# Step orders of five engines rewritten in a float32 attention kernel, on one core

## The chip, the cores and the metric

The kernel runs on one core of a Trainium2 chip. The metric is the device time of one execution in microseconds (us), as the median of several runs; lower is better. The engines of the core are named as in the profile: PE is TensorE (PEld its weight loads), DVE is VectorE, ACT is ScalarE, POOL is GpSimd, SP is SyncE, which here only issues DMAs.

## The reference

For each of 8 batches of 512 rows and 1024 columns, in float32 (the constants `EPS = 1e-6`, 16 heads of 64):

```python
scale_shift = emb @ W_emb + b_emb
scale, shift = jnp.split(scale_shift, 2, axis=-1)
xn = _rms_norm(x, g_norm) * (1.0 + scale) + shift
qkv = xn @ W_qkv
q = _rms_norm(q, g_q)
k = _rms_norm(k, g_k)
logits = jnp.einsum('bhqd,bhkd->bhqk', q, k) * d ** (-0.5)
attn = jax.nn.softmax(logits, axis=-1)
o = jnp.einsum('bhqk,bhkd->bhqd', attn, v)
return o + o @ W_out        # and x is added to it
```

## The kernel before

The work is a stream of small steps, 8 batches one behind the other, each batch with 8 pairs of heads. Precision is kept by splitting numbers in a high and a low part: a projection is three matmuls (high by high, high by low, low by high), a score or a value product is two.

What each engine does, and in which order, is written out by hand as text: three tables `HEAD` (batch 0, lines 34 to 94), `BODY` (batches 1 to 6, lines 96 to 141, run six times) and `TAIL` (batch 7, lines 143 to 180), each with one list of steps for each of the five engines. A step is named pair, letter, number: `3F2` is step F number 2 of pair 3. Pairs 8 and 9 in a table are pairs 0 and 1 of the batch that follows, so the batches overlap. A list is followed strictly; semaphores hold an engine where its next step needs another engine. The letters:

- **C** and **P** (PE, lines 500 to 502 and 525 to 527): six matmuls of a projection, 128x384 (for P 32 to 47 128x256). C is the q, k, v projection of a pair, P the output projection, which has 48 steps a batch and few companions on the other engines.
- **D** on ACT copies v and squares q and k (lines 741, 742), on DVE sums the squares (L880), on POOL adds an epsilon and takes the power -0.5 (L970, L973, 128x4 each); **M** on DVE scales q and k out of the projection bank (L886).
- **T** (PE, L553) turns q (T0) and k (T1); ACT rounds them (L696, L700), DVE makes the rest (L830, L834).
- **S** (PE, lines 590, 591): two 128x512 matmuls of scores. DVE takes the row maximum (L859), ACT the exponential with its sum (L718, two instructions). **N** on DVE: reciprocal of the sum (L863), and the scaling of the row block of `probs` in place, from SBUF to SBUF, 128x512 (L865).
- **F** (PE, L598): four 128x128 transposes of the scaled probabilities into one of two flip banks. ACT rounds them to `pt_hi` (L724), DVE subtracts to `pt_lo` (L869) and by that frees the bank. A flip (F, T or X) waits until the flip two before it has been freed (`releases`, line 238).
- **W** (PE, lines 609, 610): the two value products of an F; it waits until that F has been freed. **V** splits v for it (ACT L688, POOL L951, 128x256).
- **O** adds the two halves of a head's result (ACT L729, DVE L876). **Q** splits the pair's result: ACT rounds it (`o_hi`, L734), POOL subtracts (`o_lo`, L966, 128x512).
- **X** and **A** make the next batch's normalised input (ACT L648, L660, L666; DVE L784, L796; POOL L960, 128x512). **L** splits the weights, in batch 0 alone: ACT L643, and the remainder half on DVE (L767) and half on POOL (L933), 128x384, both with two operands in SBUF. **Y** is a step like L in batch 0 (L854). **K** and **R** add the residual (L907).

The two instructions of a W step:

```python
                        pe.wait_ge(flip_free, flip_at(order, b, "F", n, p)[0] + 1)
                        v_t = v_split[h][:, i, :]
                        nc.tensor.matmul(pv_bank[h][:, :], v_t, pt_hi[n % 2][:, :], start=(i == 0), stop=False)
                        nc.tensor.matmul(pv_bank[h][:, :], v_t, pt_lo[n % 2][:, :], start=False,
                                         stop=(i == TT - 1)).then_inc(pv_used, 1)
```

Of the kernel before, what the change touches and what calls it, by code (L numbers as in the profile page):

```python
# [50 lines left out]
        8W4 8W5 P5 P6 8F6 P7 P8 P9 8F7 8W6 9S0 9S1 P10 8W7 P11 9S2 9S3 P12 P13 P14 9S4 9S5 P15 9F0 9F1 9S6 9S7 P16 9F2
        9W0 9F3 9W1 P17 P18 9W2 9W3 P19 P20 P21 9F4 9F5 P22 P23 9F6 9F7 9W4 9W5 P24 P25 9W6 9W7 P26 P27 P28 P29 P30 P31
# [1098 lines left out]
```

## Time and profile before

| what | value |
|---|---|
| median of 3 runs | 2278.25 us (2277.76 to 2278.84) |
| the profiled execution's own time | 2278.89 us |
| its span, first to last instruction | 2276.0 us |
| PE busy | 2256.2 us (99%), 13392 matmuls |
| DVE busy | 1597.9 us (70%) |
| ACT busy | 1345.7 us (59%) |
| POOL busy | 651.7 us (29%) |
| granted TensorE clock, mean | 0.999 |

The span is what the timeline shows; the execution's own time is 2.9 us more, which lies around it. Busy time of PE is a union of matmuls whose ends are modelled, so 99% does not say that PE never waits; the starts of its instructions do.

### The profile page before, as it was taken

To read this page: it belongs to the slowest core of one execution; us is meant where nothing else is said; L and a number is where in the kernel's file an instruction comes from. 1 tells how busy PE (TensorE), PEld (TensorE's weight loads), DVE (VectorE), ACT (ScalarE), POOL (GpSimd) and SP (SyncE) were. 2 spreads that over 40 slices of the span, in tenths; PEclk is the share of its full clock that TensorE was granted. 3 is DMA by queue.
4 is the path that set the end of the run, shared out by engine and by line. 5 is a ranking of instruction groups with operands and counts; after the bars stand their busy time and mean duration, and the time that the engine had idled before them with its cause. 6 is when DMAs were issued, how large, how long until landed. Compare 5 with 4: busy or idle time off the path is not lost.

```text
span 2276.0 us, 36733 instructions
## 1 busy us (share of the span) xinstructions
PE 2256.2 (99%) x13392; PEld 2110.3 (93%) x13392; DVE 1597.9 (70%) x3284; ACT 1345.7 (59%) x3101; POOL 651.7 (29%) x880
## 2 busy tenths in 40 slices
...
GB/s 359 224 167 177 112 154 228 178 99 110 118 220 184 107 115 88 256 148 112 111 114 256 112 112 112 122 253 107 112 112 130 291 92 118 82 151 246 111 121 65
DMA packets 71269, 346.35 MB, mean 152 GB/s; under 512 B 7601, under 2 KB 43441, under 8 KB 47537
## 3 DMA queue, kind: packets, MB, share of 16 engines
...
## 4 chain that ended last, share of the span: by engine, by line
PE 86%; DVE 8%; ACT 2%; issue 1%; POOL 0%; DMA 0%; ACTq 0%; DVEq 0%
PE proj_bank L502 18%; PE proj_bank L500 18%; PE proj_bank L501 18%; PE flip_bank L598 9%; PE pv_bank L609 5%; PE pv_bank L610 5%; PE score_bank L590 4%; PE score_bank L591 4%; PE flip_bank L553 2%; DVE probs L865 2%; DVE neg_max L859 2%; DVE pt_lo L869 2%; PE flip_bank L563 1%; ACT k_hi L700 1%; PE proj_bank L525 1%
## 5 line engine op out<-in xcount | busy, mean ns | idle before, releaser
L500 PE MATMUL proj_bank<-w_split,xn_hi 128*128 128x384 f32 x2048 | 700.0, 342 | 1.4 <-DVE res L907 0.8
L502 PE MATMUL proj_bank<-w_split,xn_lo 128*128 128x384 f32 x2048 | 688.5, 336 | 0.0
L501 PE MATMUL proj_bank<-w_split,xn_hi 128*128 128x384 f32 x2048 | 687.4, 336 | 0.0
L718 ACT ACTIVATE probs<-score_bank,neg_max 128x512 f32<-128x512 f32 x512 | 352.6, 691 | 213.5 <-DVE neg_max L859 211.2
L500 PEld LDWEIGHTS proj_bank<-w_split,xn_hi 128*128 128x128 f32 x2048 | 385.2, 188 | 18.1 <-DVE xn_lo L854 1.0
L501 PEld LDWEIGHTS proj_bank<-w_split,xn_hi 128*128 128x128 f32 x2048 | 385.5, 188 | 15.2
L724 ACT CAST pt_hi<-flip_bank 128x512 fp32r<-128x512 f32 x512 | 288.8, 591 | 182.0 <-PE flip_bank L598 91.1
L869 DVE TENSOR_TENSOR pt_lo<-flip_bank,pt_hi 128x512 fp32r<-128x512 f32 x512 | 339.9, 685 | 78.1 <-ACT pt_hi L724 75.9
L502 PEld LDWEIGHTS proj_bank<-w_split,xn_lo 128*128 128x128 f32 x2048 | 384.8, 188 | 0.0
L859 DVE TENSOR_REDUCE neg_max<-score_bank 128x1 f32<-128x512 f32 x512 | 341.3, 684 | 17.0 <-PE score_bank L591 13.0
L865 DVE TENSOR_SCALAR probs<-probs,row_inv 128x512 f32<-128x512 f32 x512 | 275.7, 539 | 18.1
L598 PE MATMUL flip_bank<-ident,probs 128*128 128x128 f32 x2048 | 284.4, 273 | 1.1 <-DVE q_split L830 0.4
L598 PEld LDWEIGHTS flip_bank<-ident,probs 128*128 128x128 f32 x2048 | 242.5, 140 | 32.8 <-DVE pt_lo L869 7.3
L973 POOL TENSOR_TENSOR qk_rstd<-qk_ms_eps,neg_half 128x4 f32<-128x4 f32 x256 | 264.6, 1033 | 20.0
L970 POOL TENSOR_TENSOR qk_ms_eps<-qk_ms,eps_col 128x4 f32<-128x4 f32 x256 | 55.3, 216 | 719.2 <-DVE qk_ms L880 719.1
L609 PE MATMUL pv_bank<-pt_hi,v_split 128*128 128x512 f32 x512 | 224.3, 438 | 4.2 <-DVE pt_lo L869 4.2
L500 PE MATMUL proj_bank<-w_split,o_hi 128*128 128x384 f32 (+1 forms) x672 | 215.2, 320 | 0.0
L951 POOL TENSOR_TENSOR v_split<-v_stage,v_split 128x256 fp32r<-128x256 f32 x128 | 98.9, 773 | 401.3 <-ACT v_split L688 401.3
L502 PE MATMUL proj_bank<-w_split,o_lo 128*128 128x384 f32 (+1 forms) x672 | 213.6, 318 | 0.0
L501 PE MATMUL proj_bank<-w_split,o_hi 128*128 128x384 f32 (+1 forms) x672 | 213.5, 318 | 0.0
L590 PE MATMUL score_bank<-k_hi,q_split 128*128 128x512 f32 x512 | 206.0, 402 | 0.1
L591 PE MATMUL score_bank<-k_lo,q_split 128*128 128x512 f32 x512 | 201.6, 394 | 0.0
...
## 6 DMA issues: line engine op xcount, KB each, us to landing
...
```

Source lines behind the costliest of these rows:

```text
L500: nc.tensor.matmul(dst, a_hi, w_hi, start=(kt == 0), stop=False)
L501: nc.tensor.matmul(dst, a_hi, w_lo, start=False, stop=False)
L502: mm = nc.tensor.matmul(dst, a_lo, w_hi, start=False, stop=(kt == KT - 1))
L590: nc.tensor.matmul(score_bank[n % 2][:, :], q_t, k_hi[h][:, :], start=True, stop=False)
L591: nc.tensor.matmul(score_bank[n % 2][:, :], q_t, k_lo[h][:, :], start=False, stop=True).then_inc(score_full, 1)
L598: mm = nc.tensor.transpose(flip_bank[flip][:, qt * P:(qt + 1) * P], probs[h][:, qt, i * P:(i + 1) * P], ident[:, :])
L609: nc.tensor.matmul(pv_bank[h][:, :], v_t, pt_hi[n % 2][:, :], start=(i == 0), stop=False)
L718: nc.scalar.activation(probs[h][:, i, :], score_bank[n % 2][:, :], ACT.Exp, bias=neg_max[:, n:n + 1], accum_out=row_sum[:, n:n + 1]).then_ ...
L724: nc.scalar.copy(pt_hi[n % 2][:, :], flip_bank[flip][:, :]).then_inc(flip_hi, 1)
L859: nc.vector.tensor_reduce(neg_max[:, n:n + 1], score_bank[n % 2][:, :], AX.X, ALU.max, negate=True).then_inc(max_done, 1)
L865: nc.vector.tensor_scalar(probs[h][:, i, :], probs[h][:, i, :], row_inv[:, n:n + 1], None, ALU.mult).then_inc(probs_ready, 1)
L869: nc.vector.tensor_tensor(pt_lo[n % 2][:, :], flip_bank[flip][:, :], f32(pt_hi[n % 2][:, :]), ALU.subtract).then_inc(flip_free, 1)
```

## The change

The functions, the instructions, the jobs and the buffers stay. The text of the orders changes: each of the 14 lists that changed holds the same steps as before, in another order (in `TAIL`, the list of SyncE did not change). By its description the orders were planned with wide GpSimd steps and VectorE steps on two SBUF operands kept apart.

Cut to its core, the start of the lists of `BODY`, one place of `BODY` and `HEAD` that the prediction names, and the lists of POOL and SP in `BODY`:

```diff
 BODY = {
     "TensorE": """
         2C0 2C1 2C2 2C3 2C4 2C5 2C6 2C7 2C8 2C9 2C10 2C11 2C12 2C13 2C14 2C15 3C0 3C1 3C2 3C3 2T0 2T1 3C4 3C5 3C6 3C7
-        3C8 3C9 2S0 2S1 3C10 3C11 2S2 2S3 3C12 3C13 3C14 2S4 2S5 3C15 2F0 2F1 4C0 2S6 2S7 4C1 2F2 2F3 2W0 2W1 4C2 4C3
-        4C4 3T0 3T1 2W2 2W3 4C5 4C6 4C7 2F4 4C8 4C9 2F5 3S0 2F6 2W4 3S1 4C10 2F7 2W5 3S2 3S3 2W6 4C11 2W7 4C12 3S4 3S5
-        3F0 3F1 4C13 4C14 3F2 3W0 3F3 3W1 3S6 3S7 3W2 4C15 3W3 5C0 5C1 3F4 3F5 5C2 5C3 4T0 4T1 3W4 3W5 5C4 5C5 3F6 5C6
...
-        8S6 8F0 8F1 9C14 9C15 8F2 8F3 8W0 8W1 8S7 P0 8W2 8W3 9T0 9T1 P1 P2 P3 P4 8F4 P5 P6 8F5 8F6 8W4 9S0 9S1 8F7 8W5
...
+        3C8 3C9 2S0 2S1 3C10 3C11 2S2 2S3 3C12 3C13 3C14 2S4 2S5 3C15 2F0 2F1 4C0 2S6 4C1 2W0 2W1 2S7 2F2 2F3 4C2 4C3
+        3T0 3T1 2W2 2W3 4C4 4C5 2F4 4C6 4C7 4C8 2F5 2W4 2F6 3S0 3S1 2F7 2W5 2W6 4C9 4C10 2W7 3S2 3S3 4C11 4C12 3S4 3S5
+        4C13 3F0 3F1 4C14 3S6 3W0 3S7 3W1 3F2 3F3 4C15 5C0 3W2 3W3 5C1 3F4 3F5 5C2 5C3 4T0 4T1 3W4 3W5 5C4 5C5 3F6 5C6
...
+        9C12 8S6 8W0 8S7 8W1 8F2 8F3 9C13 9C14 8W2 8W3 9C15 8F4 8F5 P0 P1 8W4 9T0 9T1 8W5 P2 P3 P4 8F6 P5 P6 8F7 8W6 9S0
...
     "ScalarE": """
...
-        2F2 2F3 4D0 3T0 3V0 3T1 4D1 2F4 2O0 2F5 3S0 2F6 3S1 2F7 3S2 3S3 4D2 3V1 2O1 3F0 3S4 3F1 3S5 2Q0 3F2 3F3 3S6 4D3
...
+        2F3 2S7 4D0 3T0 3V0 3T1 2F4 2O0 4D1 2F5 2F6 2F7 3S0 3S1 2O1 3V1 3S2 3S3 4D2 2Q0 3S4 3F0 3F1 3S5 3F2 3F3 3S6 3S7
...
     "VectorE": """
...
-        2F6 3N1 2F7 3S2 3S3 3N2 3N3 4D2 3S4 2O1 3S5 3F0 4M2 3F1 3N4 3N5 3F2 3S6 3F3 3S7 3N6 4D3 3N7 3O0 4M3 3F4 3F5 5D0
...
+        2F7 3N0 3N1 3S2 3S3 2O1 3N2 3N3 4D2 3S4 3S5 3N4 3F0 3F1 4M2 3N5 3S6 3S7 3F2 3F3 3N6 3N7 4D3 3O0 4M3 3F4 3F5 5D0
...
     "GpSimd": """
-        0Q0 1Q0 2D0 2D1 2D2 2V0 2D3 2V1 3D0 3D1 +A0 +A1 3D2 +A2 +A3 3D3 4D0 3V0 4D1 3V1 4D2 2Q0 4D3 4V0 5D0 5D1 4V1 3Q0
-        5D2 5D3 5V0 6D0 6D1 5V1 4Q0 6D2 6D3 6V0 7D0 +X0 +X1 7D1 7D2 +X2 +X3 6V1 7D3 +X4 +X5 5Q0 8D0 +X6 +X7 8D1 8D2 7V0
-        7V1 8D3 6Q0 9D0 9D1 8V0 8V1 9D2 7Q0 9D3 9V0 9V1""".split(),
+        0Q0 1Q0 2D0 2D1 2D2 2V0 2D3 2V1 3D0 3D1 +A0 +A1 3D2 +A2 +A3 3D3 4D0 3V0 4D1 3V1 2Q0 4D2 4D3 4V0 5D0 5D1 4V1 3Q0
+        5D2 5D3 5V0 6D0 6D1 5V1 4Q0 6D2 6D3 6V0 7D0 6V1 +X0 +X1 7D1 5Q0 7D2 +X2 +X3 7D3 +X4 +X5 8D0 8D1 +X6 +X7 7V0 8D2
+        7V1 8D3 6Q0 8V0 9D0 9D1 8V1 7Q0 9D2 9D3 9V0 9V1""".split(),
     "SyncE": """
-        E2 E3 E4 3W1 E5 4W0 4W1 +X0 +X1 +X2 +X3 5W0 5W1 6W0 6W1 7W0 7W1 8W0 8W1 9W0 9W1 W0 W1 W2 W3 O0 E6 O1 E7 O2 E8 W4
+        E2 E3 E4 3W1 E5 4W0 4W1 +X0 +X1 +X2 +X3 5W0 5W1 6W0 6W1 7W0 7W1 8W0 8W1 9W0 9W1 W0 W1 W2 W3 O0 E6 O1 E7 O2 W4 E8
```

And of `HEAD`, TensorE:

```diff
-        2C12 1S4 1S5 1F0 1F1 2C13 2C14 1F2 1W0 1F3 1W1 1S6 1S7 1W2 2C15 1W3 3C0 3C1 1F4 1F5 3C2 3C3 2T0 2T1 1W4 1W5 3C4
...
+        7C12 7C13 6S6 7C14 6S7 6F0 7C15 6F1 8C0 8C1 6W0 +X2 6W1 8C2 8C3 7T0 8C4 7T1 8C5 8C6 8C7 6F2 8C8 8C9 8C10 +X3 6W2
+        7S0 7S1 6F3 8C11 6F4 6W3 6F5 6W4 6F6 7S2 7S3 8C12 6F7 6W5 6W6 8C13 8C14 6W7 7S4 7S5 8C15 7F0 7F1 7S6 9C0 7S7 9C1
```

## Rows read from the trace of the kernel before

**Rows 1.** The page: span, busy time by engine, and two groups of instructions.
```profile
span 2276.0 us, 36733 instructions
...
PE 2256.2 (99%) x13392; PEld 2110.3 (93%) x13392; DVE 1597.9 (70%) x3284; ACT 1345.7 (59%) x3101; POOL 651.7 (29%) x880
...
L724 ACT CAST pt_hi<-flip_bank 128x512 fp32r<-128x512 f32 x512 | 288.8, 591 | 182.0 <-PE flip_bank L598 91.1
...
L865 DVE TENSOR_SCALAR probs<-probs,row_inv 128x512 f32<-128x512 f32 x512 | 275.7, 539 | 18.1
```

**Rows 2.** Timeline of PE, batch 3: start us, us, engine, line, tiles, count.
```profile
1005.74 1.04 PE L598 MATMUL flip_bank<-ident,probs 128*128 128x128 f32 x8
...
1006.78 0.34 PE L501 MATMUL proj_bank<-w_split,xn_hi 128*128 128x384 f32 x1
1006.96 0.34 PE L502 MATMUL proj_bank<-w_split,xn_lo 128*128 128x384 f32 x1
...
1008.53 0.34 PE L502 MATMUL proj_bank<-w_split,xn_lo 128*128 128x384 f32 x1
```

**Rows 3.** The same timeline, around the wait of 3W2.
```profile
1010.97 0.40 PE L590 MATMUL score_bank<-k_hi,q_split 128*128 128x512 f32 x1
1011.20 0.40 PE L591 MATMUL score_bank<-k_lo,q_split 128*128 128x512 f32 x1
1012.20 0.50 PE L609 MATMUL pv_bank<-pt_hi,v_split 128*128 128x512 f32 x1 [0.60 <-DVE pt_lo L869]
```

**Rows 4.** Timelines of ACT, POOL and DVE ahead of the wait of rows 3.
```profile
1008.67 0.64 ACT L734 CAST o_hi<-o_pair 128x512 fp32r<-128x512 f32 x1
...
1009.38 1.29 POOL L966 TENSOR_TENSOR o_lo<-o_pair,o_hi 128x512 fp32r<-128x512 f32 x1 [2.10 <-ACT o_hi L734]
...
1009.38 1.58 DVE L865 TENSOR_SCALAR probs<-probs,row_inv 128x512 f32<-128x512 f32 x1
...
1011.46 0.68 DVE L869 TENSOR_TENSOR pt_lo<-flip_bank,pt_hi 128x512 fp32r<-128x512 f32 x1
```

**Rows 5.** Timelines of POOL, DVE and PE, around the wait of 8F2 in batch 3.
```profile
1154.57 1.28 POOL L966 TENSOR_TENSOR o_lo<-o_pair,o_hi 128x512 fp32r<-128x512 f32 x1 [0.69 <-ACT o_hi L734]
...
1155.12 1.02 DVE L865 TENSOR_SCALAR probs<-probs,row_inv 128x512 f32<-128x512 f32 x1
...
1157.56 0.34 PE L502 MATMUL proj_bank<-w_split,xn_lo 128*128 128x384 f32 x1
1157.98 1.25 PE L598 MATMUL flip_bank<-ident,probs 128*128 128x128 f32 x8
1158.99 0.47 PE L609 MATMUL pv_bank<-pt_hi,v_split 128*128 128x512 f32 x1
```

**Rows 6.** Waits of PEld in batch 3 (943.1 to 1221.5): total us, times, longest.
```profile
PEld flip_bank L598 <- DVE pt_lo L869: 1.1, 4, 0.4
```

**Rows 7.** The same view for batch 0 (41 to 387).
```profile
PEld flip_bank L553 <- DVE pt_lo L869: 2.3, 4, 1.8
PEld pv_bank L609 <- DVE pt_lo L869: 1.6, 3, 1.0
```

**Rows 8.** Timelines of POOL, DVE and PE in batch 0, around the wait of 8T1.
```profile
292.68 4.90 POOL L933 TENSOR_TENSOR w_split<-w_raw,w_split 128x384 fp32r<-128x384 f32 x4 [1.22 <-ACT w_split L643]
...
294.06 3.94 DVE L767 TENSOR_TENSOR w_split<-w_raw,w_split 128x384 fp32r<-128x384 f32 x3
...
296.83 0.34 PE L502 MATMUL proj_bank<-w_split,xn_lo 128*128 128x384 f32 x1
298.65 0.66 PE L553 MATMUL flip_bank<-ident,qk_stage 128*128 128x128 f32 x4 [1.48 <-DVE pt_lo L869]
```

**Rows 9.** Line L865 by itself: ns min/median/max, first and last start.
```profile
L865 DVE TENSOR_SCALAR probs<-probs,row_inv x512: 485/487/1585, 76.1 to 2240.8; 128x512 f32<-128x512 f32 x171
```

**Rows 10.** Timelines of POOL and DVE in batch 0: a power beside L865.
```profile
226.31 1.01 POOL L973 TENSOR_TENSOR qk_rstd<-qk_ms_eps,neg_half 128x4 f32<-128x4 f32 x1
...
227.13 0.49 DVE L865 TENSOR_SCALAR probs<-probs,row_inv 128x512 f32<-128x512 f32 x1
```

More of the change, by code:

```diff
@@ L51 @@
[L51 to L52 removed]
+        1C5 1C6 1C7 1C8 1C9 0S0 0S1 1C10 1C11 0S2 0S3 1C12 1C13 0S4 0S5 1C14 0F0 0F1 1C15 0S6 2C0 0W0 0W1 0S7 0F2 0F3
+        2C1 2C2 2C3 1T0 1T1 0W2 0W3 2C4 2C5 2C6 0F4 2C7 2C8 2C9 0W4 0F5 0F6 1S0 1S1 2C10 0F7 0W5 0W6 2C11 1S2 1S3 0W7
+        2C12 2C13 1S4 2C14 1S5 1F0 1F1 2C15 1S6 3C0 1W0 1W1 1S7 1F2 1F3 3C1 3C2 3C3 1W2 2T0 2T1 1W3 3C4 3C5 3C6 1F4 3C7
@@ new lines @@
+        3C8 3C9 1W4 1F5 1F6 2S0 2S1 3C10 3C11 1F7 1W5 1W6 2S2 2S3 3C12 1W7 3C13 3C14 3C15 4C0 2S4 2S5 4C1 2F0 2F1 4C2
+        2S6 4C3 2W0 2W1 3T0 3T1 2S7 4C4 4C5 4C6 4C7 2F2 4C8 4C9 2F3 2W2 3S0 2F4 3S1 2W3 2F5 4C10 2W4 2F6 3S2 4C11 3S3
+        2F7 2W5 2W6 4C12 3S4 4C13 2W7 3S5 3F0 3F1 4C14 3S6 4C15 3W0 3W1 3S7 3F2 3F3 5C0 5C1 3W2 4T0 4T1 3W3 5C2 5C3 5C4
+        5C5 5C6 3F4 3F5 4S0 4S1 5C7 3W4 3F6 3F7 3W5 5C8 4S2 3W6 4S3 5C9 3W7 5C10 4S4 5C11 4S5 5C12 4F0 4F1 4S6 4S7 5C13
+        5C14 4W0 4W1 4F2 4F3 5C15 6C0 4F4 4W2 4W3 4F5 6C1 6C2 5T0 5T1 4W4 4W5 6C3 6C4 6C5 4F6 6C6 6C7 4F7 4W6 5S0 5S1
@@ L53 @@
+        9C11 7W6 7W7 9C12 9C13 8S4 8S5 9C14 8F0 8F1 9C15 8S6 P0 8W0 8W1 8S7 8F2 8F3 P1 P2 P3 9T0 9T1 8W2 8W3 P4 P5 P6
+        8F4 P7 P8 8F5 9S0 9S1 8W4 8F6 P9 8F7 8W5 8W6 9S2 9S3 P10 8W7 P11 9S4 P12 9S5 P13 9S6 9F0 9F1 P14 P15 9W0 9W1 9S7
+        9F2 9F3 P16 P17 9W2 9W3 P18 9F4 9F5 P19 P20 9W4 9W5 9F6 9F7 P21 P22 9W6 9W7 P23 P24 P25 P26 P27 P28 P29 P30 P31
         P32 P33 P34 P35 P36 P37 P38 P39 P40 P41 P42 P43 P44 P45 P46 P47""".split(),
@@ new lines @@
+        0S1 1D2 0S2 0S3 0S4 0F0 0F1 0S5 1D3 3L0 3L1 3L2 0S6 0F2 0F3 3L3 2D0 0S7 1T0 1V0 1T1 0F4 0O0 2D1 0F5 0F6 1S0 0F7
+        1S1 2D2 0O1 1V1 1S2 1S3 0Q0 1S4 1F0 1F1 1S5 2D3 4L0 4L1 4L2 1F2 1F3 1S6 1S7 4L3 +A0 3D0 2T0 2V0 2T1 1F4 1O0 3D1
+        +A1 +A2 1F5 1F6 +A3 2S0 3D2 2S1 1F7 1O1 2V1 1Q0 2S2 2S3 3D3 5L0 5L1 5L2 2S4 2F0 2F1 2S5 5L3 4D0 2S6 3T0 3T1 2S7
+        2F2 4D1 2F3 2F4 3S0 2F5 3V0 2O0 3S1 2F6 4D2 3S2 2F7 3S3 2O1 3S4 3F0 3F1 3S5 3V1 2Q0 4D3 6L0 3S6 3F2 3S7 3F3 6L1
+        6L2 4T0 4V0 4T1 5D0 6L3 3O0 3F4 3F5 5D1 3F6 4S0 3F7 4S1 4S2 3O1 4S3 4V1 3Q0 5D2 4S4 4S5 4F0 4F1 4S6 4S7 4F2 4F3
@@ new lines @@
+        5D3 7L0 7L1 4F4 5V0 4F5 7L2 7L3 4O0 5T0 5T1 6D0 4F6 6D1 4F7 4O1 5S0 5S1 5V1 4Q0 5S2 5S3 6D2 5S4 5F0 5F1 5S5 5S6
+        5F2 5S7 5F3 6D3 5F4 6V0 5O0 5F5 6T0 6T1 7D0 5F6 5F7 6S0 7D1 6S1 5O1 +X0 6V1 5Q0 6S2 6S3 7D2 6S4 6S5 +X1 6F0 7D3
+        6F1 6S6 6S7 +X2 8D0 7T0 7T1 6F2 8D1 +X3 6F3 6F4 7S0 7S1 7V0 8D2 6F5 6O0 6F6 6F7 7S2 7S3 6O1 7V1 7S4 7S5 7F0 7F1
+        8D3 L0 L1 L2 7S6 7F2 7S7 7F3 L3 9D0 6Q0 8T0 8V0 8T1 7O0 9D1 7F4 7F5 8S0 8S1 7F6 7F7 9D2 8S2 7O1 8S3 8V1 7Q0 8S4
+        8F0 8F1 8S5 9D3 L4 L5 L6 8S6 8F2 8F3 L7 8S7 9T0 9V0 9T1 8F4 8O0 8F5 8F6 9S0 9S1 8F7 9S2 8O1 9S3 9V1 9S4 9F0 9F1
@@ new lines @@
+        9S5 9S6 L8 L9 L10 L11 9F2 9F3 9S7 9O0 9F4 9F5 9F6 9F7 9O1""".split(),
+    "VectorE": """
+        X0 Y0 X1 1L0 1L1 1L2 Y1 X2 0D0 1L3 0M0 Y2 X3 0D1 0M1 Y3 0D2 0M2 0D3 2L0 0M3 2L1 2L2 1D0 2L3 0T0 1M0 0T1 1D1 0S0
+        0S1 1M1 0N0 0N1 0S2 1D2 0S3 0N2 1M2 0N3 0S4 0S5 0N4 0F0 0F1 0N5 1D3 0S6 3L0 3L1 3L2 1M3 0F2 0F3 0S7 2D0 3L3 0N6
+        0N7 1T0 2M0 1T1 0F4 2D1 0O0 2M1 0F5 0F6 1S0 1S1 1N0 0F7 1N1 2D2 1S2 1S3 0O1 2M2 1N2 1N3 1S4 1S5 1N4 1F0 1F1 1N5
+        2D3 1S6 1S7 4L0 4L1 4L2 1F2 1F3 2M3 4L3 1N6 1N7 3D0 2T0 +A0 3M0 2T1 1F4 3D1 1O0 3M1 2S0 1F5 1F6 2S1 2N0 +A1 3D2
+        2N1 1F7 +A2 3M2 +A3 1O1 2S2 2S3 2N2 2N3 3D3 2S4 2S5 5L0 5L1 5L2 2F0 2F1 3M3 2S6 4D0 5L3 2N4 2N5 4M0 3T0 2S7 2N6
+        3T1 2F2 4D1 2N7 2F3 3S0 4M1 2F4 3S1 3N0 2F5 2O0 3N1 2F6 3S2 4D2 3S3 3N2 2F7 4M2 3N3 3S4 3S5 2O1 3N4 3F0 3F1 3S6
+        4D3 3S7 6L0 3N5 3F2 4M3 3F3 6L1 6L2 4T0 3N6 3N7 4T1 5D0 3O0 6L3 3F4 3F5 5M0 4S0 5D1 4S1 3F6 4N0 3F7 5M1 4N1 4S2
+        4S3 4N2 3O1 4N3 4S4 4S5 5D2 4N4 4N5 4F0 4F1 5M2 4S6 4S7 4N6 4N7 4F2 4F3 5D3 +B0 7L0 7L1 5M3 4F4 4F5 7L2 4O0 5T0
+        7L3 5T1 4F6 6D0 6D1 4F7 6M0 5S0 5S1 6M1 4O1 5N0 5N1 5S2 5S3 I0 5N2 5N3 6D2 5S4 5S5 6M2 5N4 5F0 5F1 5N5 5S6 5S7
+        5N6 5F2 5N7 5F3 6D3 5F4 6M3 5O0 5F5 6T0 6T1 5F6 7D0 5F7 6S0 7M0 6S1 +X0 7D1 6N0 6N1 5O1 7M1 6S2 6S3 6N2 6N3 7D2
+        6S4 6S5 +X1 7M2 6S6 6N4 6N5 6S7 6F0 7D3 6F1 6N6 6N7 +X2 7M3 8D0 7T0 8M0 7T1 6F2 8D1 +X3 8M1 7S0 7S1 6F3 6F4 7N0
+        8D2 6F5 6O0 6F6 8M2 7N1 7S2 6F7 7S3 7N2 7N3 7S4 7S5 6O1 7N4 7N5 7F0 7F1 8D3 7S6 7S7 L0 L1 L2 7F2 8M3 7F3 L3 9D0
+        7N6 8T0 9M0 7N7 8T1 9D1 7O0 7F4 8S0 7F5 9M1 8S1 8N0 I1 8N1 7F6 7F7 8S2 8S3 9D2 8N2 7O1 8N3 9M2 8S4 8S5 8N4 8F0
+        8F1 8N5 9D3 8S6 L4 L5 L6 9M3 8F2 8F3 8S7 R0 L7 8N6 8N7 9T0 9T1 R1 8F4 8O0 8F5 9S0 9S1 8F6 I2 9N0 8F7 9N1 9S2 9S3
+        9N2 R2 9S4 8O1 9N3 9N4 9S5 9S6 9F0 9F1 9N5 R3 9N6 L8 L9 L10 9S7 9F2 9F3 L11 9N7 9F4 9F5 R4 9F6 9F7 R5 R6 R7 R8
@@ L89 @@
-        L4 L5 L6 L7 9V0 9V1 L8 L9 L10 L11""".split(),
+        X1 1L0 1L1 X3 1L2 0D0 1L3 X5 0D1 X7 0D2 0D3 0V0 2L0 1D0 2L1 2L2 2L3 0V1 1D1 1D2 3L0 1D3 3L1 3L2 3L3 2D0 1V0 2D1
+        2D2 1V1 0Q0 4L0 2D3 4L1 4L2 +A0 4L3 2V0 3D0 3D1 +A1 +A2 +A3 3D2 2V1 1Q0 5L0 3D3 5L1 5L2 5L3 4D0 4D1 3V0 4D2 3V1
+        2Q0 4D3 6L0 6L1 6L2 4V0 6L3 5D0 5D1 4V1 3Q0 5D2 5D3 7L0 5V0 7L1 7L2 7L3 6D0 6D1 5V1 4Q0 6D2 6D3 6V0 7D0 7D1 +X0
+        6V1 +X1 7D2 5Q0 +X2 +X3 7D3 +X4 8D0 +X5 8D1 +X6 +X7 7V0 8D2 7V1 L0 8D3 L1 L2 L3 9D0 8V0 6Q0 9D1 9D2 8V1 7Q0 L4
@@ new lines @@
+        7C3 5F7 7C4 7C5 7C6 +X0 5W7 6S0 6S1 7C7 7C8 +X1 7C9 6S2 6S3 7C10 7C11 6S4 6S5 7C12 7C13 +X2 7C14 6S6 6S7 7C15
+        8C0 8C1 6F0 8C2 8C3 6F1 8C4 7T0 6W0 6W1 7T1 8C5 8C6 6F2 8C7 8C8 8C9 +X3 6W2 7S0 7S1 6F3 8C10 8C11 6F4 7S2 6W3
+        6F5 7S3 6W4 6F6 8C12 6F7 6W5 7S4 7S5 6W6 8C13 6W7 7F0 7F1 8C14 7S6 8C15 7W0 7W1 7S7 7F2 7F3 9C0 9C1 8T0 7W2 8T1
+        7W3 9C2 9C3 7F4 9C4 9C5 9C6 7F5 7W4 7F6 8S0 8S1 7F7 7W5 7W6 9C7 9C8 7W7 8S2 8S3 9C9 9C10 8S4 8S5 9C11 8F0 8F1
+        9C12 8S6 8W0 8S7 8W1 8F2 8F3 9C13 9C14 8W2 8W3 9C15 8F4 8F5 P0 P1 8W4 9T0 9T1 8W5 P2 P3 P4 8F6 P5 P6 8F7 8W6 9S0
@@ L122 @@
+        6V0 5O0 5F5 5F6 6T0 6T1 5F7 7D0 5O1 6V1 +X0 6S0 6S1 7D1 5Q0 6S2 6S3 7D2 +X1 6S4 6S5 6S6 6S7 7D3 +X2 6F0 8D0 6F1
+        7T0 7T1 6F2 8D1 +X3 6F3 7S0 6F4 7S1 8D2 7V0 6F5 7S2 6O0 6F6 7S3 6F7 7S4 7F0 7F1 7S5 6O1 7V1 8D3 7S6 6Q0 7F2 7S7
+        7F3 8T0 8V0 8T1 7F4 9D0 7O0 7F5 7F6 7F7 8S0 8S1 9D1 7O1 8V1 8S2 8S3 7Q0 8S4 8F0 8F1 8S5 9D2 8F2 8F3 8S6 8S7 8O0
+        9D3 8F4 8F5 9V0 9T0 9T1 8F6 8F7 9S0 9S1 8O1 9V1 9S2 9S3 9F0 9S4 9F1 9S5 9S6 9F2 9S7 9F3 9F4 9O0 9F5 9F6 9F7 9O1""".split(),
     "VectorE": """
@@ new lines @@
+        5F0 5F1 5N5 6D2 5S6 5S7 6M2 5N6 5F2 5N7 5F3 6D3 5F4 5O0 5F5 6M3 5F6 6T0 6T1 5F7 7D0 +X0 7M0 6S0 6S1 5O1 6N0 6N1
+        7D1 6S2 6S3 +X1 7M1 7D2 6S4 6N2 6N3 7M2 6S5 6N4 6N5 6S6 6S7 +X2 6N6 7D3 6N7 7M3 6F0 8D0 6F1 7T0 8M0 7T1 6F2 8D1
+        +X3 8M1 7S0 7S1 6F3 7N0 6F4 7S2 8D2 7S3 6F5 7N1 7N2 6F6 8M2 7N3 6F7 7S4 6O0 7S5 7N4 7F0 7F1 7N5 7S6 6O1 8D3 7S7
+        7N6 7F2 8M3 7F3 7N7 8T0 8T1 7F4 9D0 7O0 7F5 9M0 7F6 8S0 8S1 7F7 8N0 8N1 9D1 8S2 8S3 9M1 7O1 8N2 8N3 8S4 8S5 8N4
+        8F0 8F1 8N5 9D2 8S6 8S7 8F2 8F3 9M2 8N6 8N7 8O0 9D3 8F4 8F5 9M3 9T0 R0 9T1 8F6 8F7 9S0 9S1 R1 9N0 9N1 8O1 9S2
@@ new lines @@
+        2W2 3T1 2W3 4C3 4C4 2F4 4C5 4C6 4C7 2F5 2W4 2F6 3S0 3S1 2F7 2W5 2W6 4C8 4C9 2W7 3S2 3S3 4C10 4C11 3S4 3S5 4C12
+        3F0 3F1 3S6 4C13 3S7 4C14 3W0 3W1 3F2 3F3 4C15 5C0 3F4 3W2 3W3 3F5 5C1 3W4 4T0 5C2 4T1 3W5 5C3 5C4 3F6 5C5 5C6
+        3F7 3W6 4S0 4S1 5C7 3W7 5C8 4S2 5C9 4S3 5C10 4S4 5C11 4S5 5C12 4S6 4F0 4F1 5C13 5C14 4W0 4W1 4S7 4F2 4F3 5C15
+        6C0 4F4 4W2 4W3 4F5 6C1 4W4 5T0 6C2 5T1 4W5 6C3 6C4 4F6 6C5 6C6 4F7 4W6 5S0 5S1 6C7 4W7 6C8 5S2 6C9 5S3 6C10 5S4
+        6C11 5S5 6C12 5S6 5F0 5F1 6C13 6C14 5W0 5W1 5S7 5F2 5F3 6C15 7C0 5F4 5W2 5W3 5F5 7C1 5W4 6T0 7C2 6T1 5W5 7C3 7C4
```

133 lines of the change are left out of this document (38 added, 95 removed).

## Prediction

> **What bounds the kernel now.** I read the page first. PE is busy for 2256.2 of 2276.0 us, DVE, the next, for 1597.9 [rows 1]. So the span is PE's stream of 13392 matmuls, and only two things can change it: the pace of the stream, and the places where PE stands still. Neither is seen in PE's busy share, because a matmul's end is modelled. Both are seen in the starts, so I read PE's timeline.
>
> The pace: nine projection matmuls of 384 columns start from 1006.96 to 1008.53 [rows 2], 0.174 us each, and a C or P step of six takes 1.05 us. A matmul of 512 columns takes 0.23 (1010.97 to 1011.20) [rows 3], an S or W step 0.46. Eight transposes and one projection matmul fill 1005.74 to 1006.78 [rows 2]; less 0.17 that is 0.87, so an F step of four costs 0.44. Wherever PE's starts stand further apart than this, it waited.
>
> The waits: in batch 3 there are two places of weight. **3W2**: the last score matmul starts at 1011.20, the value product should start at 1011.43 and starts at 1012.20 [rows 3]: 0.77 us. **8F2**: after the projection matmul of 1157.56 the flips should start at 1157.74 and start at 1157.98, and these eight take 1.01 us up to the next start where 0.87 is their price [rows 5]: 0.24 + 0.14, some 0.4. All waits of PEld for `pt_lo` at flips in this batch come to 1.1 us in four [rows 6], which holds 8F2; weight loads run up to a quarter of a microsecond ahead of their matmuls, so PE itself loses less. I put the batch at 0.77 + 0.4 + 0.4 for the small ones, 1.6 us. The same two places come back in all six body batches, whose text is the same.
>
> What was late there? At 3W2 it is `pt_lo`, started at 1011.46, behind a probability scaling (N step, L865) that took 1.58 us [rows 4]. The smallest and the median of the 512 such steps are 485 and 487 ns [rows 9]. In the very moment in which it began, 1009.38, POOL began `o_lo` (Q step), 1.29 us; the scaling took these 1.29 and then its own 0.3 to 0.5 [rows 4]. At 8F2 the scaling took 1.02, beside an `o_lo` that had begun 0.55 earlier and ended 0.15 before it [rows 5]. So a scaling that meets a wide POOL step waits for it. The mean of 539 against 487 [rows 1, 9] is 0.052 x 512 = 27 us of DVE time lost so, of which most hides behind other work. In batch 0 the weight splits do it too: three on DVE fill 3.94 us beside four on POOL in 4.90, and PE, which last started at 296.83, starts 8T1 only at 298.65 [rows 8], 1.65 us late. Waits for `pt_lo` alone are 2.3 and 1.6 us of that batch [rows 7].
>
> **The change, part by part.**
>
> *Steps and neighbours.* Each list holds the same steps, so PE's work is the same. Other neighbours cost little: eight flips in front of a projection cost 2 x 0.44 [rows 2], and flips in front of a value product about that. By count, flips stand in front of a projection 34 times in place of 21 in a body batch (41 for 31 in HEAD, 26 for 11 in TAIL), 103 more in all; S or W stand in front of one 90 times less. At an estimated 0.01 us each the two nearly cancel. I take **+0.5**, bounds 0 and +1.5.
>
> *Collisions in the body.* I read the new ScalarE list for what stands in front of each Q, because POOL starts `o_lo` some 0.07 us after that cast (1008.67 + 0.64, then 1009.38) [rows 4]. Before, 2Q0 stood behind the exponential 3S5, with N4 and N5 of pair 3 just due on DVE. Now it stands behind 4D2 and ahead of 3S4: N2 and N3 of pair 3 are due before the cast ends, and N4 needs an exponential and a reciprocal first, in which most of the 1.29 us goes by. 7Q0 moves likewise, from behind 8S4 to behind 8S3, in front of the exponential that frees N4. So both waits of the body lose their cause: 6 x (0.77 + 0.4) = **-7.0**. Bounds: none of it (0), and all waits of the body, 6 x 1.6 = -9.6.
>
> *Less room elsewhere.* The new lists put W closer behind its F. I counted the PE work between an F and its own W with the prices above: under 2.2 us in 9 cases of a body batch (3 before), under 2.5 in 14 (4 before); under 3, 35 of 64 (20 before). The least that the hand-off takes is the cast, 0.59 [rows 1], plus `pt_lo`, 0.68 [rows 4], and three hand-overs, some 1.6 together. So 2F6 to 2W6, with 3S0 3S1 2F7 2W5 between, has 0.3 us to spare, and only if ACT and DVE have nothing else in front; DVE has 4M1 there. Of the four short cases of before one waited, because of the collision. I charge 0.4 us a batch in place of the 0.4 of small waits, and 0.2 on top, since the count of short ones tripled: 6 x 0.2 = **+1.2**. Bounds: 0, and nine cases at 0.3, 6 x 2.7 = +16.
>
> *HEAD.* L steps now stand with other DVE work between. Of the 3.9 us of waits for `pt_lo` [rows 7] and the others I take back 3.3: 1.65 at 8T1, 0.8 at 1W2 (the 1.0 of rows 7 less the load's lead), the rest small. But three hand-offs are shorter than 1.6: 6F4 to 6W4 has 6W3 and 6F5 between, 0.90 us, 0.7 short; 6F3 to 6W3 1.5; 4F7 to 4W7 1.4. I charge 1.0. Together **-2.3**, bounds -6 and +3.
>
> *POOL's and SP's queues.* 8D2 now queues behind 7V0, up to 0.9 us; its power feeds M, which frees a projection bank that is needed four C steps later at the least, 4.2 us, so nothing. 6V1 goes ahead of X. On SP, W4 (weights for the third output job) goes ahead of a residual load: earlier, not later. TAIL has no wait worth a term. All **0**; if 8D2 came late it would show as a wait for `qk_stage`.
>
> The sum against the profiled span: -7.0 + 1.2 - 2.3 + 0.5 = -7.6, 2276.0 to about 2268.4. That execution took 2278.89, 0.6 above the median of 2278.25, so I round the gain down to 7.3 and forecast **2271.0**.
>
> A rule that speaks against it. In the trace a scaling takes 0.49 us while POOL is in a power of 1.01 us [rows 10], so a narrow step does not hold DVE up. The Trainium skill (SBUF — State Buffer, on the engine side's ports) has the shared pair as an exclusive lock, held by whichever of the two engines starts first for the whole instruction. By that the powers would block as well, and keeping only wide steps apart would move collisions onto them; the trace disagrees for the power.
>
> **The rivals.**
> *A, scalings are not in the plan.* "Two SBUF operands" may mean two inputs. Such DVE steps, splits of weights, are in batch 0 alone; the scaling has one tensor input. Then body collisions fall where they fall: -2.3 + 0.5, and the body as before: 2276.5. Against it: both body Qs that hurt have moved away. For it: nothing else in the body would need planning, yet its lists changed throughout, as a new search would change them. 20%.
> *B, slower: the short hand-offs run out.* Place: the F to W pairs under 2.2 us, 2F6, 3F0, 5F4, 6F1, 6F4, 7F6, 8F0, 9F4, 9F6. If each costs 0.3 us, a body batch loses 2.7 and gains 1.2 + 0.4: +1.1, six times +6.6, with HEAD at 0: 2285. It decides from 0.2 us per case on. For it: DVE is busy for 70% of the span on average [rows 1] and for more in the dense parts, so a queue of one step is common. Against it: before, three of the four short ones passed. 12%.
> *C, collisions move to the powers.* By the row there is no such block, so the chance is small; as a mechanism it would give the 1.2 us a batch back: 2278. 5%.
> The forecast has 63%.
>
> **How the numbers follow.** 0.2% is 4.6 us, about what a measurement of this kernel can tell from no change. Faster by more, under 2273.7: nearly all of the forecast and little of A, 0.64. Within: A, C, the weak end of the forecast, 0.24. Slower: B, 0.12. The range goes from all collisions gone with small charges (-7.6 less 5, 2265) to where half of B is in, 2281.
>
> **What would show it.** Right: PE's waits at 3W2 and 8F2 are gone from every body batch; L865's mean falls from 539 towards 490 and its longest below 1 us; a body batch falls from 278.4 (1221.5 less 943.1, the window of rows 6) to about 277.4. Wrong: L865's mean stays above 520 (A), or the waits of PEld for `pt_lo` at L609 grow in number beyond ten a batch (B), or L865 grows beside L973 (C).

## The result and the profile after

The changed kernel takes 2288.55 us, the median of 6 runs (2287.01 to 2289.27), against 2277.96 for the kernel before in the same runs: a ratio of 1.0045, 95% interval 1.0032 to 1.0058. It is slower by 10.6 us, where I had forecast 7 us less and a range up to 2281.

The page of the changed kernel, with the lines that answer to [rows 1] (in the changed kernel the code lines have numbers one lower: L864 is the scaling that was L865, L965 is `o_lo`, L868 is `pt_lo`; in runs that add lines the numbers are higher again):

```profile
span 2285.4 us, 36733 instructions
...
PE 2260.7 (99%) x13392; PEld 2109.6 (92%) x13392; DVE 1590.7 (70%) x3284; ACT 1345.3 (59%) x3101; POOL 646.4 (28%) x880
...
L864 DVE TENSOR_SCALAR probs<-probs,row_inv 128x512 f32<-128x512 f32 x512 | 274.3, 536 | 18.1
```

The busy times say little: PE's count is the same, DVE and POOL do a few microseconds less. The mean of a scaling is 536 ns where it was 539. So the collisions have not gone. Line L864 by itself, as in [rows 9], has the same median and a longer longest:

```profile
L864 DVE TENSOR_SCALAR probs<-probs,row_inv x512: 485/487/1611, 75.3 to 2247.9; 128x512 f32<-128x512 f32 x171
```

Where the time came from is seen by cutting PE's timeline where the first matmul of each batch's first C step starts; the last stretch runs to the end of the span. The whole change of the span is +9.4 us:

| stretch | before | changed | difference |
|---|---|---|---|
| up to the end of HEAD | 386.24 | 384.34 | -1.9 |
| a body batch | 278.2 to 278.6 | 280.1 to 280.2 | +1.7 each, +10.3 in six |
| TAIL | 219.40 | 220.38 | +1.0 |

The waits of PEld in batch 3 (944.4 to 1224.5), the view of [rows 6], have changed in kind: total, times, longest.

```profile
PEld score_bank L589 <- ACT probs L717: 1.9, 3, 0.8
PEld flip_bank L597 <- issue: 1.1, 2, 0.6
PEld pv_bank L608 <- issue: 0.9, 2, 0.7
PEld proj_bank L499 <- DVE qk_stage L885: 0.4, 1, 0.4
```

The flips' wait for `pt_lo` of 1.1 us in [rows 6] is no longer there, nor is the wait of 3W2. In their place scores wait for exponentials (S steps), and flips and value products wait for something that this view does not name ("issue" is time in which it sees no releaser). So I walked through the places where PE's starts stand too far apart. The timelines of PE, DVE and POOL around the first of them, step 5F0:

```profile
1062.88 0.34 PE L501 MATMUL proj_bank<-w_split,xn_lo 128*128 128x384 f32 x1
1063.42 0.96 PE L597 MATMUL flip_bank<-ident,probs 128*128 128x128 f32 x7 [0.20 <-DVE probs L864]
...
1061.58 0.15 DVE L862 RECIPROCAL row_inv<-row_sum 128x1 f32<-128x1 f32 x1
1061.77 1.50 DVE L864 TENSOR_SCALAR probs<-probs,row_inv 128x512 f32<-128x512 f32 x1
...
1061.68 1.30 POOL L965 TENSOR_TENSOR o_lo<-o_pair,o_hi 128x512 fp32r<-128x512 f32 x1 [0.45 <-ACT o_hi L733]
```

The flips should have started at 1063.05 and start at 1063.42, 0.37 late. They read the four scalings of the head, and the last, 5N3, took 1.50 us: `o_lo` of 4Q0 had begun 0.09 us before it. It is the picture of [rows 4], at another pair. The same at 8N3, with 7Q0:

```profile
1153.27 0.16 DVE L862 RECIPROCAL row_inv<-row_sum 128x1 f32<-128x1 f32 x1
1153.47 1.48 DVE L864 TENSOR_SCALAR probs<-probs,row_inv 128x512 f32<-128x512 f32 x1
...
1153.38 1.29 POOL L965 TENSOR_TENSOR o_lo<-o_pair,o_hi 128x512 fp32r<-128x512 f32 x1 [1.34 <-ACT o_hi L733]
...
1154.44 0.34 PE L501 MATMUL proj_bank<-w_split,xn_lo 128*128 128x384 f32 x1
1155.10 1.07 PE L597 MATMUL flip_bank<-ident,probs 128*128 128x128 f32 x8 [0.32 <-DVE probs L864]
...
1157.30 0.40 PE L590 MATMUL score_bank<-k_lo,q_split 128*128 128x512 f32 x1
1157.95 0.47 PE L608 MATMUL pv_bank<-pt_hi,v_split 128*128 128x512 f32 x1 [0.26 <-DVE pt_lo L868]
```

8F0 comes 0.49 late (1154.61 was due), and 8W0 0.42 (1157.53 was due), since everything behind the scaling on DVE is late too. The third is 6N3, beside `xn_lo` of an X step, which is as wide as `o_lo`; behind it the row maximum and the exponential that 6S7 waits for are late, and PE loses 0.40 between 1098.61, the last matmul of 6S6, and 1099.24, the first of 6S7 (the expectations below call this place 6S6):

```profile
1095.84 1.60 DVE L864 TENSOR_SCALAR probs<-probs,row_inv 128x512 f32<-128x512 f32 x1
...
1095.88 2.72 POOL L959 TENSOR_TENSOR xn_lo<-y_half,xn_hi 128x512 fp32r<-128x512 f32 x2
...
1098.61 0.40 PE L590 MATMUL score_bank<-k_lo,q_split 128*128 128x512 f32 x1
1099.24 0.50 PE L589 MATMUL score_bank<-k_hi,q_split 128*128 128x512 f32 x1 [0.23 <-ACT probs L717]
```

A fourth place is no collision. PE waits for an exponential at 7S2, 0.83 us late (four flips take 0.36 up to the next start, so 1119.61 was due), and in ACT's queue that exponential, 7S0, stands behind the step +X3: a cast of its first half, four 128x128 slices of the second half, the cast of that half; then comes the cast of 6F3. ACT had stood idle for 3.37 us ahead of +X3, until DVE had made its `y_half`.

```profile
1119.25 0.60 PE L597 MATMUL flip_bank<-ident,probs 128*128 128x128 f32 x4
1120.44 0.50 PE L589 MATMUL score_bank<-k_hi,q_split 128*128 128x512 f32 x1 [0.59 <-ACT probs L717]
...
1116.54 0.62 ACT L665 CAST xn_hi<-y_half 128x512 fp32r<-128x512 f32 x1 [3.37 <-DVE y_half L795]
1117.06 1.50 ACT L659 ACTIVATE y_half<-flip_bank,mod_now 128x128 f32<-128x128 f32 x4
1118.60 0.62 ACT L665 CAST xn_hi<-y_half 128x512 fp32r<-128x512 f32 x1
1119.12 0.58 ACT L723 CAST pt_hi<-flip_bank 128x512 fp32r<-128x512 f32 x1
1119.60 0.69 ACT L717 ACTIVATE probs<-score_bank,neg_max 128x512 f32<-128x512 f32 x1
```

### The profile page after: what moved, and what is told of

Read it like the earlier page. It is cut to its first block, busy times and chain, and to the rows that moved or that the text cites. A ratio compares the mean times of both kernels' runs of the same rounds, so it can differ in the third digit from the quotient of the medians.

```text
span 2285.4 us, 36733 instructions
## 1 busy us (share of the span) xinstructions
PE 2260.7 (99%) x13392; PEld 2109.6 (92%) x13392; DVE 1590.7 (70%) x3284; ACT 1345.3 (59%) x3101; POOL 646.4 (28%) x880
## 4 chain that ended last, share of the span: by engine, by line
PE 91%; DVE 6%; ACT 1%; issue 1%; DMA 0%; SPq 0%; ACTq 0%; DVEq 0%
PE proj_bank L501 19%; PE proj_bank L499 19%; PE proj_bank L500 19%; PE flip_bank L597 9%; PE pv_bank L608 5%; PE pv_bank L609 5%; PE score_bank L589 4%; PE score_bank L590 4%; PE flip_bank L552 2%; DVE probs L864 2%; DVE neg_max L858 2%; DVE y_half L795 1%; PE flip_bank L562 1%; PE proj_bank L620 1%; PE proj_bank L524 1%
## 5 line engine op out<-in xcount | busy, mean ns | idle before, releaser
L868 DVE TENSOR_TENSOR pt_lo<-flip_bank,pt_hi 128x512 fp32r<-128x512 f32 x512 | 343.7, 687 | 77.5 <-ACT pt_hi L723 73.4
L864 DVE TENSOR_SCALAR probs<-probs,row_inv 128x512 f32<-128x512 f32 x512 | 274.3, 536 | 18.1
L608 PE MATMUL pv_bank<-pt_hi,v_split 128*128 128x512 f32 x512 | 217.5, 425 | 3.8 <-DVE pt_lo L868 3.8
L609 PE MATMUL pv_bank<-pt_lo,v_split 128*128 128x512 f32 x512 | 201.6, 394 | 0.0
## 6 DMA issues: line engine op xcount, KB each, us to landing
emb_stage<-in_w_emb SPq DMA_DIRECT2D x5, 1024.0 KB, 10.6
```

Source lines behind the costliest of these rows:

```text
L864: nc.vector.tensor_scalar(probs[h][:, i, :], probs[h][:, i, :], row_inv[:, n:n + 1], None, ALU.mult).then_inc(probs_ready, 1)
L868: nc.vector.tensor_tensor(pt_lo[n % 2][:, :], flip_bank[flip][:, :], f32(pt_hi[n % 2][:, :]), ALU.subtract).then_inc(flip_free, 1)
```

## The experiments

Theory 1: the body is slower because scalings collide with wide GpSimd steps at places where the hand-off to PE has no room. Theory 2, my rival B: the new order leaves too little work between F and W, collision or not. "Before" in the ratios is the kernel before, timed beside the run. A gap at a place is told as the start of a PE matmul less the start that was due by the prediction's pace.

**Two waits in the changed kernel (a_qhold).** A small table names the scaling that POOL's step is to wait for; nothing else is touched.

```diff
+HOLD = {"HEAD": {}, "BODY": {"4Q0": "5N3", "7Q0": "8N3"}, "TAIL": {}}
...
+                    until = HOLD["HEAD" if order is HEAD else "TAIL" if order is TAIL else "BODY"].get(step)
+                    if until is not None:
+                        hp, _, _, hn = read_step(until)
+                        pool.wait_ge(probs_ready, (b * PAIRS + hp) * 8 + hn + 1)
```

> The changed kernel with one addition in BODY: GpSimd waits, ahead of o_lo of 4Q0 and of 7Q0, until VectorE has finished the scaling 5N3 and 8N3. Theory 1 (collisions): in the changed kernel these two scalings took 1.5 us beside an o_lo that began about 0.1 us before them, and PE's waits at 5F0 (0.39), 8F0 (0.51) and 8W0 (0.47) follow from that; with the wait both scalings take 0.49, and a body batch falls by 1.37 us from 280.1 to 278.7: 2288.5 - 8.2 = 2280.3. Theory 2 (short hand-offs): PE waits there because the new order leaves too little work between F and W; the collision goes but less than 0.3 us a batch comes back: 2287 or more.

Measured: 2279.40 us, 1.0005 of before (0.9996 to 1.0014). A body batch takes 278.7 (278.60 to 278.77), and HEAD and TAIL are as in the changed kernel. The scaling 5N3 and its neighbour on POOL:

```profile
1059.02 0.49 DVE L871 TENSOR_SCALAR probs<-probs,row_inv 128x512 f32<-128x512 f32 x1
...
1059.58 1.27 POOL L976 TENSOR_TENSOR o_lo<-o_pair,o_hi 128x512 fp32r<-128x512 f32 x1 [1.10 <-DVE probs L871]
```

The scaling is back at 0.49 and POOL starts behind it. PE's gaps at 5F0, 8F0 and 8W0 are gone, and a body batch takes 1.40 us less. Of the 10.6 us over the kernel before 0.9 are left: Theory 1, and not Theory 2, whose 2287 is far off.

**The same for the X step and for TAIL (a_qxhold).** The table above with `"+X2": "6N3"` added in BODY and `"2Q0": "3N3"` in TAIL.

> As the run before, and the same kind of wait ahead of xn_lo of +X2 (until 6N3) in BODY and ahead of o_lo of 2Q0 (until 3N3) in TAIL. Theory 1: PE's waits at 6S4, 6S5 and 7C12 (0.19 + 0.26 + 0.11) and at 6S6 (0.39 + 0.11) follow from the 1.6 us scaling 6N3, and the one of TAIL at 3F0 (0.8) from 3N3; 6 x 1.06 + 0.8 = 7.2 us less than the run before: 2273. Half of the 1.06 may stay, since at 6S6 an exponential behind an input step of 2.7 us on ScalarE is late as well: then 2276. Theory 2: as the run before, within 1 us.

Measured: 2274.99, 0.9985 of before (0.9975 to 0.9994). A body batch takes 278.17, 0.55 less than in the run before; TAIL 219.56 in place of 220.41. PE's wait ahead of 6S7 is gone, as are those of TAIL ahead of 3F0 and 3S6 (0.17 and 0.62). The waits from 6S4 to 7C12 (0.19, 0.26, 0.12) are the same as with the collision: they come before 6N3 and had been wrongly put on its account, so 2273 was too low. Not every collision is gone: 6N0 beside +X1 still takes 0.74, and 6N5 now meets +X3 and takes 1.17 to 1.18, with no gap of PE behind it.

**The cure on the kernel before (b_qhold).** `"2Q0": "3N5", "7Q0": "8N4"` in BODY.

> The kernel before with the same kind of wait in BODY, at its own two collisions: o_lo of 2Q0 waits until the scaling 3N5 is done, o_lo of 7Q0 until 8N4. Theory 1: 3W2 (0.77 + 0.10) and 8F2 (0.24 + 0.21) no longer wait, 1.3 us a batch: 2278.0 - 7.9 = 2270. Theory 2: the waits of PE were only uncovered there and move to the next short hand-off: 2275 or more.

Measured: 2270.39, 0.9963 of before (0.9948 to 0.9978). A body batch takes 277.0, 1.38 less than 278.4. PE's score and value products at 3W2, in its timeline:

```profile
1009.46 0.39 PE L598 MATMUL score_bank<-k_lo,q_split 128*128 128x512 f32 x1
1009.69 0.40 PE L616 MATMUL pv_bank<-pt_hi,v_split 128*128 128x512 f32 x1
1009.92 0.39 PE L617 MATMUL pv_bank<-pt_lo,v_split 128*128 128x512 f32 x1
```

0.23 us each, where [rows 3] had 1.00 between the first two. So the price that the prediction gave the two old collisions, 1.2 us a batch, was about right, and they were worth 8 us; the change just put others in their place. No gap of PE above 0.1 us is left in batch 3. Yet 5N2 and 7N5 still take 1.14 and 1.32 there, beside 4Q0 and 6Q0: a collision costs something only where its scaling is waited for.

**Only HEAD (h_head).** The table HEAD of the changed kernel with BODY and TAIL of the kernel before.

> The kernel before with the table HEAD of the changed kernel; BODY and TAIL as before. By the two traces HEAD ends 1.9 us earlier in the changed kernel, which had started 0.3 late: 2278.0 - 2.2 = 2275.8 if the tables don't act on each other. If the gain of HEAD was only work pushed into the first body batch, 2278.

Measured: 2277.05, 0.9993 (0.9983 to 1.0002). The body batches are those of before (278.2 to 278.8) and TAIL is 219.4. The gain of HEAD in medians, 1.5 us, cannot be told from none by this interval. In the traces the stretch from the kernel's first flip to the end of HEAD takes 350.4 us before, 348.2 in the changed kernel and 349.3 here: with the old BODY behind it the new HEAD keeps only half of its gain, so the tables do act on each other.

**The order alone (a_qmove).** In the changed kernel's ScalarE list of BODY:

```diff
-5V1 5S3 4Q0 5S4 5F0
+5V1 5S3 5S4 4Q0 5F0
...
-8S2 8S3 7Q0 8S4 8F0
+8S2 8S3 8S4 7Q0 8F0
```

> The changed kernel with two steps of the ScalarE list of BODY moved by one place, no wait added: 4Q0 behind the exponential 5S4 in place of ahead of it, 7Q0 behind 8S4. Then o_lo begins some 0.9 us later, when 5N3 and 8N3 are over. Theory 1 (a collision is a matter of which of two steps begins first): as with the waits, a body batch of 278.7 in place of 280.1, 2279.4 in all. If only an explicit wait keeps them apart, because VectorE is late for the next scaling too: a collision with 5N4 or 8N4 and 2285 or more.

Measured: 2281.43, 1.0017 (1.0007 to 1.0026), a body batch of 279.0 to 279.2. The mean of a scaling falls to 512 ns, exactly as with the two waits. So both collisions are gone with the order alone. But a body batch is 0.36 us slower than with the waits, 2 us in all: PE's timeline shows that 8W0 is still late, 0.37 between 1156.28 and 1156.88. No collision is left there; by the lists the cast of `o_hi`, 0.6 us, now stands in front of the cast of 8F0. So this one short hand-off of Theory 2 does run out once a cast stands in its way.

```profile
1156.28 0.40 PE L590 MATMUL score_bank<-k_lo,q_split 128*128 128x512 f32 x1
1156.88 0.47 PE L608 MATMUL pv_bank<-pt_hi,v_split 128*128 128x512 f32 x1 [0.20 <-DVE pt_lo L868]
```

**A narrow step in the same place (a_narrow).**

```diff
+                        cols = slice(0, 4) if order is BODY and p in (4, 7) else slice(0, T)
-                        nc.gpsimd.tensor_tensor(o_lo[:, p % PAIRS, :], o_pair[:, :], f32(o_hi[:, p % PAIRS, :]),
+                        nc.gpsimd.tensor_tensor(o_lo[:, p % PAIRS, cols], o_pair[:, cols], f32(o_hi[:, p % PAIRS, cols]),
```

> The changed kernel, in which o_lo of 4Q0 and 7Q0 of BODY is computed for its first 4 columns alone (the rest of these two pairs' low parts is left out); orders and waits are those of the changed kernel. Theory 1: a step of some 0.2 us holds nobody up for long, 5N3 and 8N3 take 0.49 to 0.6 and a body batch 278.7: 2279.4. Theory 3 (it is not the length of the GpSimd step but that VectorE's scaling is slow beside anything on GpSimd): 5N3 and 8N3 stay above 0.8 us, 2283 or more.

Measured: 2279.17, 1.0005 (0.9996 to 1.0015), a body batch of 278.7, the mean of a scaling 512. No order and no wait differs from the changed kernel here, just the width of two POOL steps. This separates the collision itself from any side effect of a wait. The POOL step in place of the one at 1061.68, and the scaling 5N3 beside it, which again began 0.09 us later:

```profile
1059.69 0.20 POOL L966 TENSOR_TENSOR o_lo<-o_pair,o_hi 128x4 fp32r<-128x4 f32 x1 [0.45 <-ACT o_hi L733]
...
1059.78 0.48 DVE L864 TENSOR_SCALAR probs<-probs,row_inv 128x512 f32<-128x512 f32 x1
```

**One more wait in HEAD (b_best).** As b_qhold, with `"0Q0": "1N5"` in HEAD.

> The kernel before with the two waits of BODY (2Q0 until 3N5, 7Q0 until 8N4) and one in HEAD: o_lo of 0Q0 waits until 1N5. Theory 1: 1N4 takes 0.49 in place of 1.58, PE's wait at 1W2 (0.77 + 0.11) goes: 2270.4 - 0.9 = 2269.5. If the waits of HEAD hide one behind another, 2270.4.

Measured: 2270.62, 0.9966 (0.9954 to 0.9978): nothing against b_qhold. In the trace 1N4 is back at half a microsecond and the gap of PE at 1W2 falls from 0.77 to 0.07, while HEAD ends 0.8 us earlier (386.49 against 387.33), of which 0.2 is an earlier start. The kernel's first flip starts anywhere from 35.6 to 37.2 us in these profiles, so a gain of 0.6 us in a stretch that runs once is not to be had from medians.

**The best of both (h_best).** HEAD of the changed kernel, BODY and TAIL of the kernel before, with the two waits of b_qhold.

> HEAD of the changed kernel, BODY and TAIL of the kernel before with the two waits of BODY: HEAD's gain of 1.5 to 2.2 us and BODY's of 8.1 should add up, 2277.05 - 8.1 = 2269.0.

Measured: 2269.22 (2267.31 to 2270.23), 0.996 of before (0.9946 to 0.9974). It beats both kernels, by 9 and 19 us; against b_qhold the difference of 1.2 us is not settled. In its trace too HEAD is 1.2 us shorter than before, not 2.2.

**What was left over: the X step (a_xshort, with a control b_xshort).** With its three costly collisions kept off, a body batch of the new order still takes 278.17, where that of the old order takes 277.0.

```diff
-                for i in range(4):
+                for i in range(1 if r in (1, 3) and n >= 2 * TT else 4):
```

> The changed kernel with its collisions removed (as in the run with waits at 4Q0, 7Q0, +X2 and 2Q0), in which ScalarE's share of +X1 and +X3 in BODY is cut from four to one of the 128x128 slices (three quarters of the upper half of these rows' input is left out): the step takes some 1.4 in place of 2.7 us. Theory 4: PE's wait of 0.83 at 7S2 in each body batch is for the exponential 7S0, which stands behind +X3 in the ScalarE list; it goes, and a body batch falls from 278.17 to 277.3, 2270 in all. The wait at 6S4 and 6S5 (0.46), which ScalarE's +X1 does not precede, stays. If 7S2 waits for VectorE's row maximum instead, nothing moves: 2275.

> Control: the kernel before with its two waits in BODY, and the same cut in +X1 and +X3. There pair 7 has T0 and T1, five steps, between +X3 and its first exponential, and PE has no wait behind +X: a body batch stays within 0.15 of 277.0, and the whole at 2270.4, if Theory 4 is right and the cut is not simply less work for everyone.

Measured: a_xshort 2271.59 (0.9969, interval 0.9956 to 0.9983), a body batch of 277.6; b_xshort 2269.89 (0.9961, 0.9947 to 0.9974), 276.8 to 277.2. The wait at 7S2 is gone in the first, those from 6S4 to 7C12 stay, and the control moves by 0.1 us a batch. Theory 4 holds in its place, but just 0.6 of the 0.83 us came back: the next score, 7S3, now waits 0.24. The cut moves POOL's steps too. In the control +X2 now meets 6N0, which takes some 1.64 in place of 0.65, and still no gap above 0.11 us follows.

## Why the prediction was wrong

**The reading of the bound, the pace and the old waits: right.** The batch's two waits were the two collisions, and b_qhold measured 1.38 us a batch where the sum had 0.77 + 0.4. Both are gone from the changed kernel, as said. Nothing stands behind the 0.4 us of "small ones": in batch 3 of b_qhold no gap above 0.1 us is left. One reading of [rows 5] was off: the `o_lo` ended at 1155.85 and the scaling at 1156.14, 0.29 later and not 0.15.

**The step that failed: "Collisions in the body".** It read: "So both waits of the body lose their cause: 6 x (0.77 + 0.4) = -7.0". That was true, and it was the wrong question. I looked whether the collisions that hurt would go, and not which new ones would come. I had followed 2Q0 and passed 7Q0 in half a sentence; 4Q0 and the X steps I did not follow at all. Scalings above 0.6 us in a body batch went from six to four, but each of the three large ones loses 1.0 to 1.1 us, and they stand where the flips of the same head, or the next scores, are due. By the runs they cost 1.40 (Q) and 0.55 (X) us a batch. The term was -7.0 and came out as 6 x (-1.38 + 1.40 + 0.55), or +3.4, with a further +0.8 at 3N3 in TAIL, to which I had given nothing. For 7Q0 the argument named N4, which the exponential behind the cast holds back; the one in reach was N3, whose data are ready before the cast ends, and which DVE reaches only after 9M1, 7O1 and 8N2. To start behind `o_lo` by 0.09 us is enough to lose a microsecond.

**"Less room elsewhere": right that room was short, wrong where.** I counted only F to W and charged +1.2. None of the nine cases named waits by itself in the body; 8W0 does, behind the collision. What waits is scores: 7S2 by 0.83 behind +X3, and 6S4 to 7C12 by 0.57 together. Between the two orders without their costly collisions (a_qxhold and b_qhold) the runs leave 1.15 us a batch, +7 in all. I never put the X step, 2.7 us of ACT without a break, against the exponential behind it; in the old ScalarE list ten steps stand between them, in the new one 6F3 alone. The cause of the 0.57 was not tested. By the trace DVE has 6N1, 7D1 and the maximum 6S2 back to back ahead of it, and before them 6N0, which took 0.74 beside `xn_lo` of +X1: up to 0.25 us of it may be one more collision.

The batch then closes: -1.38 + 1.40 + 0.55 + 1.15 is +1.7, as measured. The last term is a difference of these same runs, so of it only the 0.6 us behind 7S2 have an experiment of their own.

**HEAD: right in sum, by luck.** -2.3 forecast, -1.9 in the trace, -2.2 from its first step on. I took back 3.3 and charged 1.0; the trace has more of both. Gone are the waits at 8T1 (1.64, [rows 8]), 1W2 (0.76), 2F2 (0.59) and 1C8 (0.41); new or longer are those at 6W3 (1.45), 9W2 (0.88 for 0.15), 3W2 (0.47), 6F4 (0.43), 2T0 (0.30) and 4W7 (0.24). The largest, 6W3, I had counted as a hand-off 0.1 us too short, and that is not what it waits for. Timelines of the changed kernel, PE and then ACT:

```profile
277.43 0.66 PE L597 MATMUL flip_bank<-ident,probs 128*128 128x128 f32 x4 [0.27 <-ACT y_half L659]
279.29 0.50 PE L608 MATMUL pv_bank<-pt_hi,v_split 128*128 128x512 f32 x1 [1.21 <-DVE pt_lo L868]
...
275.35 0.62 ACT L665 CAST xn_hi<-y_half 128x512 fp32r<-128x512 f32 x1 [3.85 <-DVE y_half L795]
275.88 1.50 ACT L659 ACTIVATE y_half<-flip_bank,mod_now 128x128 f32<-128x128 f32 x4
277.41 0.62 ACT L665 CAST xn_hi<-y_half 128x512 fp32r<-128x512 f32 x1
277.93 1.07 ACT L723 CAST pt_hi<-flip_bank 128x512 fp32r<-128x512 f32 x2
```

6W3 needs the cast of 6F3, which stands behind the same +X3 step as 7S0 does in the body. That is a reading of the trace; no run changes +X3 in HEAD.

**The rivals.** A said that body collisions "fall where they fall" and gave that nothing; it was nearest in kind, its sign came (a mean of 536, above 520), and it lacked that six repetitions of a worse place are a cost. Whether the plan counted the scaling as a step on two SBUF operands is open: misses of 0.09 us fit a plan whose durations are a little off as well as one that never looked. B had the sign and nearly the time (2285), but that was luck: its mechanism fell with a_qhold, its sign (more than ten waits for `pt_lo` at the value products) did not come, and in the body only 8W0 showed it, in a_qmove. C did not happen: 41 scalings of the changed kernel start while nothing but a power runs on POOL, and they take 487 ns on average, 490 at most.

**The rule of the Trainium skill** (SBUF — State Buffer, engine side), that whichever engine starts first keeps the shared pair for its whole instruction, is what these traces show for wide steps: 1.50 us beside 1.30. For the power of 1.0 us the traces still disagree with it. The step of 0.20 us in a_narrow decides nothing: only 0.11 us of it was left when the scaling began, and a scaling that waits loses some 0.2 us less than the rest of the POOL step (below).
